# Delta-rule layers on one core: a loop turn of four heads instead of eight

## What is computed

```python
q, k = softmax(q), softmax(k); beta = sigmoid(beta)     # 8 heads, width 32
def step(W, inp):
    qt, kt, vt, bt = inp
    wk = einsum('bhde,bhe->bhd', W, kt)
    v_new = bt * (vt - wk)
    W = W + einsum('bhd,bhe->bhde', v_new, kt)
    return W, einsum('bhde,bhe->bhd', W, qt)
```

## Time and profile before

| | us |
|---|---|
| median of three runs | 5363.59 |
| lowest, highest | 5357.72, 5369.23 |
| profiled execution | 5342.08 |
| its span | 5340.3 |
| first delta-rule layer, from 333 to 1104 us | 771.0 |
| second delta-rule layer, from 1482.5 to 2475 us | 992.5 |

### The profile page before, as it was taken

The page is one execution under the profiler, slowest core; times in us unless marked ns, Lnnn a source line. Parts: engine busy times, 40 slices in busy tenths (PEclk is TensorE's granted clock), DMA queues, the critical chain, the costliest instruction groups (busy, mean ns, idle before and its releaser), DMA issues. The chain is left out here.

```text
span 5340.3 us, 166254 instructions
## 1 busy us (share of the span) xinstructions
PE 4097.5 (77%) x71052; PEld 2447.9 (46%) x71053; DVE 2742.2 (51%) x5139; ACT 1867.5 (35%) x3387; POOL 874.9 (16%) x2195
## 2 busy tenths in 40 slices
PE   3677667679965555556788887699999999985995
PEld 1235555534344444444345555245455454443663
DVE  3444444330233322333578887388686886864343
ACT  1121111112211111111366665167575775741221
POOL 0000000000000000000255554011111111102112
PEclk7787777779966666667899998799999999996997
DMA  1000000000000000000100000000000000005223
GB/s 42 2 8 3 3 3 3 4 19 0 0 10 5 5 5 5 5 5 5 38 1 1 1 1 1 10 1 0 1 0 1 1 0 1 0 3 194 86 85 101
DMA packets 47646, 87.35 MB, mean 16 GB/s; under 512 B 7120, under 2 KB 38128, under 8 KB 46064
## 3 DMA queue, kind: packets, MB, share of 16 engines
q1 hardware_dynamic: 40944, 61.84, 3.4%
q0 software_dynamic: 6144, 16.79, 1.0%
HBM read 45.05 MB, written 33.55 MB: 15 GB/s over the span
## 5 line engine op out<-in xcount | busy, mean ns | idle before, releaser
L1656 PE MATMUL psum<-hm_ex,hm_mix 128*128 128x512 f32 x1024 | 510.1, 621 | 42.5 <-ACT hm_Aq L1736 38.5
L1722 ACT ACTIVATE hm_ex<-psum,hm_nm 128x1024 f32<-128x1024 f32 x256 | 285.6, 1116 | 296.2 <-DVE hm_nm L1780 296.1
L658 PE MATMUL psum<-fw_M,fw_qkTc 32*32 32x32 f32 x8192 | 134.4, 236 | 283.4 <-issue 283.4
L1790 DVE TENSOR_SCALAR_CACHE_REDUCE hm_plus<-hm_Aq,hm_cbcol,hm_sums 128x1024 f32<-128x1024 f32 x256 | 340.6, 1330 | 0.0
L1795 DVE COPY hm_A<-psum 128x1024 f32<-128x1024 f32 x256 | 312.9, 1222 | 51.4 <-PE psum L1665 48.1
L1656 PEld LDWEIGHTS psum<-hm_ex,hm_mix 128*128 128x128 f32 x1024 | 175.5, 191 | 351.2 <-issue 343.4
L1780 DVE TENSOR_REDUCE hm_nm<-psum 128x1 f32<-128x1024 f32 x256 | 311.1, 1215 | 11.5 <-PE psum L1644 11.5
L1665 PEld LDWEIGHTS psum<-K,hm_Aq 128*128 128x128 f32 x2048 | 236.7, 140 | 149.9 <-issue 145.3
L665 PE MATMUL psum<-fw_w,fw_stage 128*128 128x512 f32 (+1 forms) x512 | 290.7, 707 | 16.0 <-DMA fw_w<-in_slow 16.0
L1727 ACT ACTIVATE hm_junk<-hm_Aq 128x1024 f32<-128x1024 f32 x256 | 270.6, 1057 | 30.3
L1644 PE MATMUL psum<-hm_kt,hm_qd 64*32 64x512 f32 x4096 | 278.3, 602 | 0.0
(11 more groups left out here) (365 smaller groups left out, 8116.0 us busy)
## 6 DMA issues: line engine op xcount, KB each, us to landing
ex_rows_in<-ex_zero SPq DMA_DIRECT2D x2, 5120.0 KB, 24.6
ex_xs<-ex_rows_in SPq DMA_DIRECT2D x80, 128.0 KB, 2.0
ex_rows_out<-ex_ys SPq DMA_DIRECT2D x80, 128.0 KB, 1.7
ex_w<-in_ex_w SPq DMA_DIRECT2D x2, 4096.0 KB, 21.2
X<-in_x SPq DMA_DIRECT2D x2, 2048.0 KB, 12.3
out_y<-X SPq DMA_DIRECT2D x2, 2048.0 KB, 9.0
ff_w<-in_ff_w SPq DMA_DIRECT2D x2, 1024.0 KB, 5.7
pt_w_proc<-in_pt_proc SPq DMA_DIRECT2D x1, 2048.0 KB, 7.7
```

What stands on the lines that cost most here:

```text
L658: mm = pe.matmul(to(n)[rows(b), :], by(n)[rows(b), :], of(n)[rows(b), :], start=start and (stop or n == 0), stop=stop)
L1656: mm = pe.matmul(bank[4 + c], mix[:, u, :], ex[:, u, 512 * c:512 * c + 512], start=True, stop=True)
L1722: act.activation(ex[:, u, :], flat2(psum[:, 2 * u:2 * u + 2, :]), ACT.Exp, bias=nm[:, u:u + 1], accum_out=rsum[:, u:u + 1]).then_inc(s_ex, 1)
L1790: dve.tensor_scalar(plus[:, :], Aq[:, u, :], cbcol[:, :], sums[:, :], ALU.add, ALU.add, accum_out=sums[:, :]).then_inc(s_run, 1)
```

## The change

A turn of the loop now works four of the eight heads of a tile. The 32 tiles become NU = 64 units; even and odd units take the two halves of a tile, and the state tile `M` has two halves used in turn. `w` is laid out by half on the host, with q, k, v and beta of four heads in one block of 388 columns, so one projection group per unit takes the place of two per tile, and `stage` is refilled every second unit. The solution keeps its steps (`u0`, `r0`, `rk`, `rk`, `U`). ScalarE copies the half state into `Mc`, which the solving matmuls read. VectorE's three maskings of the gram become one instruction of three times the columns. Some steps change their place in the order on VectorE and ScalarE. The engines other than TensorE have a loop of 30 turns with two units in each; TensorE has the loop of 30 with a second hardware loop of two inside it, whose body is one unit.

```diff
-        def bodies(body, eng, start=None):
+        def units(body, eng, start=None):
             for i in range(-1, 2):
-                body(i, i + 1 < NT, i >= 0, i >= 1)
-            with eng.Fori(2, NT - 1) as i:
+                body(i, i // 2, i % 2, True, i >= 0, i >= 1)
+            with eng.Fori(1, NT - 1) as j:
                 if start:
                     start()
-                body(i, True, True, True)
+                for a in range(2):
+                    body(j * 2 + a, j, a, True, True, True)
             if start:
                 start()
-            for i in range(NT - 1, NT + 1):
-                body(i, i + 1 < NT, i < NT, True)
+            for i in range(NU - 2, NU + 1):
+                body(i, i // 2, i % 2, i + 1 < NU, i < NU, True)
...
 # TensorE
                 def tiles(to, by, of, sig, start=True, stop=True):
-                    for n in range(HEADS):
+                    for n in range(G):
                         for b in range(B):
...
-                def project(i, lo, hi, to, sig):
+                def project(a):
                     for h in range(CH):
-                        mm = pe.matmul(bank[to][:, 0:hi - lo], stage[:, h, :], w[:, h, lo:hi],
+                        mm = pe.matmul(bank[0][:, 0:WN], stage[:, h, :],
+                                       w[:, h, bass.ds(a, 1), :].rearrange("p a n -> p (a n)"),
                                        start=(h == 0), stop=(h == CH - 1))
...
-                    if nxt:
-                        project(i + 1, QKN, 3 * C + HEADS, 1, s_pv)
                     if ch:
+                        pe.wait_ge(s_z1, i + 1)
                         pe.wait_ge(s_l2t, i + 1)
                         pe.sem_inc(s_go, 1)
                         fourth()
...
-                bodies(body, pe)
+                for i in range(-1, 2):
+                    body(i, i // 2, i % 2, True, i >= 0, i >= 1)
+                with pe.Fori(1, NT - 1) as j:
+                    with pe.Fori(0, 2) as a:
+                        body(j * 2 + a, j, a, True, True, True)
+                for i in range(NU - 2, NU + 1):
+                    body(i, i // 2, i % 2, i + 1 < NU, i < NU, True)
...
 # ScalarE
+                        act.wait_ge(s_m, i if since(i, 1) else 1)
+                        act.activation(flat(Mc[:, :, :]), flat(M[:, a, :, :]), ACT.Copy).then_inc(s_mc, 1)
...
 # VectorE
                 def lower(i):
                     dve.wait_ge(s_ga, i + 1)
-                    own.mark(dve.tensor_tensor(l8[:, :, :], pairs[:, :, 1, :], small(1), ALU.mult))
-                    own.done(dve.tensor_tensor(l8t[:, :, :], pairs[:, :, 1, :], small(0), ALU.mult))
-                    dve.tensor_tensor(zl[:, 0, :, :], small(2), l8t[:, :, :], ALU.subtract).then_inc(s_l8, 1)
-                    dve.tensor_tensor(loff[:, :, :], pairs[:, :, 1, :], off, ALU.mult).then_inc(s_lo, 1)
+                    dve.tensor_tensor(lows[:, :, :, :], pairs[:, :, 1, :].unsqueeze(1).broadcast_to([P, 3, G, STEP]),
+                                      parts, ALU.mult).then_inc(s_l8, 1)
+                    dve.wait_ge(s_l8, i + 1)
+                    dve.tensor_tensor(zl[:, 0, :, :], small(2), l8t, ALU.subtract).then_inc(s_z1, 1)
...
                     if rc:
                         solution(r, 2, rk, s_rk)
+                    if nxt:
+                        less_max(i + 1)
                     if ch:
                         second(i)
                     if rc:
                         solution(r, 3, rk, s_rk)
-                    if nxt:
-                        less_max(i + 1)
                     if ch:
                         fourth(i)
                     if rc:
                         solution(r, 4, U, s_u)
-                    if ch:
-                        factor(i)
                     if nxt:
                         sums(i + 1)
                     if rc:
-                        state(r)
+                        state(r, 1 - a)
+                    if ch:
+                        factor(i)
```

More of the change, by code:

```diff
@@ L600, in fast_weight_stage @@
[L600 to L605, removed]
+        eb = sb("eb", [P, 3, G]); power = sb("power", [P, 2, G])
@@ new lines, in fast_weight_stage @@
+        qk = sb("qk", [P, QKN]); qkT = sb("qkT", [P, 2 * G, STEP]); vh = sb("vh", [P, CG])
+        kc = sb("kc", [P, CG]); qkTc = sb("qkTc", [P, 2 * G, STEP]); vhc = sb("vhc", [P, CG])
+        compact = lambda n: sb(n, [P, G, STEP])
+        l2, l4, z2, z3, nt, qm = (compact(n) for n in "l2 l4 z2 z3 nt qm".split())
+        lows = sb("lows", [P, 3, G, STEP])
+        l8t, l8, loff = (lows[:, y, :, :] for y in range(3))
+        u0, r0, rk, U, Mc, att = (compact(n) for n in "u0 r0 y0 U Mc att".split())
@@ new lines, in fast_weight_stage @@
+        zl = sb("zl", [P, 2, G, STEP]); M = sb("M", [P, 2, G, STEP])
+        names = ("w power staged pj dif exp root qk ga l8 z1 qm t l2 l2t l4 z2 z3 nt cv ct mc ck th rd u0 "
+                 "so r0 rk u m up in att ot fin go dch pch").split()
+        (s_w, s_power, s_staged, s_pj, s_dif, s_exp, s_root, s_qk, s_ga, s_l8, s_z1, s_qm, s_t, s_l2, s_l2t, s_l4, s_z2,
+         s_z3, s_nt, s_cv, s_ct, s_mc, s_ck, s_th, s_rd, s_u0, s_so, s_r0, s_rk, s_u, s_m, s_up,
+         s_in, s_att, s_ot, s_fin, s_go, s_dch, s_pch) = (k.sem(f"s_{n_}_{n}") for n in names)
@@ L650, in _ @@
                 pool.wait_ge(s_power, 2)
-                bodies(body, pool, own.clear)
+                units(body, pool, own.clear)
             @block.tensor
@@ L739, in body @@
                         pe.wait_ge(s_ck, r + 1)
+                        pe.wait_ge(s_m, r + 1)
                         pe.sem_inc(s_go, 1)
[L741 to L746, removed]
+                        tiles(to(5), lambda n: kc[:, cols(n)], of(U), s_up)
+                        tiles(to(6), of(qm), of(U), s_in, start=False)
                     if ch:
                         pe.wait_ge(s_z3, i + 1)
-                        pe.wait_ge(s_lo, i + 1)
                         pe.sem_inc(s_go, 1)
-                        product(z3, loff)
+                        tiles(to(3), of(loff), of(z3), s_t)
                     if rc:
@@ L835, in softmax @@
                         dve.wait_ge(s_ck, i)
-                    own.done(dve.tensor_tensor(groups(qk[:, :]), groups(ex[:, :]), wide(rs[:, :], 16), ALU.mult))
+                    own.done(dve.tensor_tensor(groups(qk[:, :]), groups(ex[:, :]), wide(rs[:, :], 2 * G), ALU.mult))
                     if since(i, 1):
@@ L909, in body @@
                         softmax(i + 1)
-                dve.memset(M[:, :, :], 0.0).then_inc(s_m, 1)
+                dve.memset(M[:, :, :, :], 0.0).then_inc(s_m, 1)
                 dve.wait_ge(s_m, 1)
-                bodies(body, dve, own.clear)
+                units(body, dve, own.clear)
 @stage
@@ L2350, in layout @@
         cols = [w[:, DH * q:DH * q + DH].reshape(C, C) for q in range(3)] + [w[:, 3 * DH]]
-        out[f"slow{n}"] = rows(np.concatenate(cols, 0).T)
+        part = lambda g: np.concatenate([c.reshape(2, -1, C)[g] for c in cols], 0)
+        out[f"slow{n}"] = rows(np.concatenate([part(1), part(0)], 0).T).reshape(P, CH, 2, -1)
         out[f"fo{n}"] = rows(a["L2_attn_fw_out_w"][n].T)
```

153 lines of the change are left out of this document (75 added, 78 removed).

## The result

The changed kernel takes 4944.49 us in the median of four runs (4932.16 to 4950.56), the kernel before 5363.41 us (four runs). The ratio is 0.9216, with a 95% interval of 0.9195 to 0.9237. 4850 us were predicted, with a range of 4740 to 5090. The trace of the changed kernel spans 4945.4 us, 394.9 less than the one before.

The account below looks back on a forecast made before the run. TensorE's instruction fetch was taken to bound both delta-rule layers; at 625 us each, 513 us less than before, the profiled 5342 us becomes 4829, plus 21.5 for the median: 4850 us, range 4740 to 5090.

Parts of the forecast that it names:

- The bound of before: Both delta-rule layers, 1763.5 us together: a turn is bound by how fast TensorE's instructions are brought in.
- The half-size body stays: TensorE's new loop body, some 860 instructions, stays with the engine: no packets after the first pass, both branches 0.2 us.
- a bound in the body's length between 715 and 1,700: TensorE loop bodies: 715 instructions repeat free of packets, 1,700 only every second time; 860 is far nearer the first.
- Rivals A and A': TensorE's inner branch: instructions fetched again for every unit (A, 6027 us, 6%) or every other unit (A', 5439 us, 4%).
- A unit at the full clock: One unit of the new loop, instructions already there, takes 9.3 us; 8.3 is the lower bound.
- The layout of 8.7 us ahead of the branch: TensorE's steps in a unit, from reading the state to the transposition, end at 8.7 us; branch and register work to 9.1.
- GpSimd's power: Within a unit: done by 7.5 us even if 4 columns take the 1.64 us of 8, so it costs nothing.
- The clock: In the new loops: 2.4 GHz nearly throughout, since no idle stretch exceeds 0.7 us.
- the forecast's own case: A unit of 8.7 to 10.4 us gives 4778 to 4982 us for the whole; chance 61%.
- rival B: Clock stays at 1.2 GHz or latency holds narrow steps: unit 10.4 to 11.8 us, 5102 us at 11.4; chance 23%.
- The sum: Per layer 28 us ahead, 34 behind, 5 first pass, 558 loop: 625 us; both 1250, 513 less than before.
- The signs named beforehand: Few dozen packets per layer, 0.2 us inner branch, equal layers, clock above 0.9, VectorE about 13 us a tile.

Follow-up runs that it names:

- experiment 5: Changed kernel with TensorE's inner loop written out as a two-unit body, plus 29 small matmuls ahead of the second layer's bodies: 4777.48 us, ratio 0.8938.
- experiment 1: Changed kernel with TensorE's inner loop written out, so its loop body is two units: 5303.94 us, ratio 0.9851.
- the four fillers: Changed kernel with four matmuls of constants into an unused bank per unit, three ahead of waits, one at the end: 4817.48 us, ratio 0.8952.
- experiment 2: Kernel before with 42 small matmuls (168 TensorE instructions) issued once ahead of the second delta-rule layer's bodies: 5041.16 us, ratio 0.9349.

## Why the prediction was right, step by step

**The bound of before.** Right. TensorE's instruction packets set the pace of both layers: 64 instructions more ahead of the first loop cost 222 us, and 120 in the same place gain 762.

**The half-size body stays.** Right in its result: no packets, branches of 0.2 us, two equal layers. The reason given, a bound in the body's length between 715 and 1,700, was too coarse. 1,721 instructions stay in experiment 5, and 1,703 stay, stay at times or never, by where they lie. What counts is how many stretches of 256 the body touches. The half body touches at most five wherever it lies, which is why the result was safe. Rivals A and A' did not come about; experiment 1's second layer shows what A would have been like, 35.0 us a pair (38.2 were set against it).

**A unit at the full clock.** 9.3 us were laid out; 8.9 are measured in the changed kernel's own units at a clock of 1.00, 9.03 with the four fillers, and 8.65 in the two-unit body, where the inner branch is gone too. The layout of 8.7 us ahead of the branch was thus good to 0.1. GpSimd's power takes 1.01 us for four columns, under the 1.64 that was allowed for, and stays hidden.

**The clock.** This was the term that was mis-sized. "2.4 GHz nearly throughout" rested on no idle stretch being over 0.7 us. The grant was 0.84 and the unit 10.2 us, 0.9 over the forecast, with stretches of only 0.4 to 0.8 us idle in it. That is near the upper end of the forecast's own case (8.7 to 10.4) and just short of rival B's (10.4 to 11.8). Rival B named the clock or latency; the fillers show that it was the clock.

**The sum.** The loop took 60 x 10.2 = 612 us, against 558; head and tail of a layer took 33 + 37 us against 28 + 34 + 5. A layer took 684 and 681 us against 625: 115 us over for the two, of which the unit makes some 108. The forecast gain of 513 us became 398.5. Part of this miss is hidden in the median by luck: the forecast added 21.5 us, by which the profiled execution before lay under its median, and the changed kernel's profiled execution (4947.25 us) lies 2.8 above its own. So 4829 was 118 us short of the profiled execution, and 4850 only 94 short of the median.

**The signs named beforehand.** Packets, branches and equal layers came as named. PE was busy for 81% of the loop (80 forecast, though for the full clock; the lower one lengthens the matmuls). VectorE was busy for 11.2 us a tile, not 13. The granted clock was 0.84, not above 0.9.

**What the prediction did not ask** is what a kept turn of full width would take, although its own rows held it: the packet-free turn of 14.1 us, partly at the lower clock, against 18.6 forecast for a tile after the change. The change brings the code's size down and pays for it in width; moving the loop by 120 instructions brings the same and pays nothing.

## What to carry to other kernels

When TensorE is idle for "issue" in a loop of many small matmuls, look at the instruction queue and the duration of the loop's branch before touching the arithmetic, and compare equal loops that lie at different places. Count the body in stretches of 256 instructions from where the gaps fall; if it only just runs into one too many, move it with a few harmless instructions, and only then think of shrinking it, since narrower groups have half the work to cover each wait (here 3.5 us more a tile, up to 0.4 of it for the order). Such a placement holds only until code ahead of it changes, so it has to be looked up in the trace again each time.

## What the runs showed of the hardware

- A TensorE loop of 1,703 instructions ran at 13.8, 20.8, 23.4, 31.0, 31.3 or 32.6 us a turn by its place in the program alone. Kept turns in a row of one to four in one and the same loop (experiment 2) show that in the marginal place it is decided turn by turn; by what is not shown.
- Two loops with equal busy shares of 81% were granted clocks of 0.84 and 1.00, and one matmul of 0.39 us at the end of each unit took some 120 us off the kernel.
